# A graph layer's neighbour sums: gathered rows as three bfloat16 pieces, two dense blocks more, one-hots made three steps ahead

## The reference

```python
m_data = x[src] @ W_data.T + b_data
m_ctrl = x[src] @ W_control.T + b_control
msg = where(edge_type == 0, m_data, m_ctrl)
agg = segment_sum(msg, dst, num_segments=12500)
y   = x + relu(agg + x @ W_self.T + b_self)
out = (y - mean(y)) / sqrt(var(y) + 1e-5)        # per node, over the 128 features
```

## Time and profile before

| | |
|---|---|
| median of three runs | 3986.37 us (3984.35 to 3987.94) |
| the profiled execution | 3988.85 us |
| its span, first to last instruction | 3987.1 us |
| mean granted TensorE clock | 0.816 |
| busy share PE, POOL, DVE, ACT | 66%, 43%, 41%, 32% |
| DMA queue of the indirect gathers | 119.78 MB, 11.4% of 16 engines |

### The profile page before, as it was taken

One profiled execution on the slowest core, in us unless ns is written; L12 is line 12 of the kernel. 1 busy time (PEld: TensorE's weight loads), 2 busy tenths in 40 slices (PEclk: granted clock), 3 DMA queues, 4 the chain that ended last, 5 costly groups with the idle time before them and its releaser, 6 DMA issues.

```text
span 3987.1 us, 50434 instructions
## 1 busy us (share of the span) xinstructions
PE 2650.9 (66%) x19115; PEld 1498.6 (38%) x19115; DVE 1623.9 (41%) x3683; ACT 1267.6 (32%) x2283; POOL 1715.3 (43%) x1815
## 2 busy tenths in 40 slices
PE   3566676666766677666666666667666666767666
PEld 2333343333433344333333334334333333333334
DVE  7434344334443344434344343434334343443332
ACT  4233232333323333333333333333333333323332
POOL 6434444344443444444344443444444344444432
PEclk9878788888887888888787888878888787888878
DMA  5111111111111111111111111111111111111110
GB/s 163 50 32 34 35 32 37 32 36 35 34 36 32 36 34 37 34 34 36 33 36 34 34 35 34 35 35 34 36 34 36 32 36 34 34 37 31 37 34 26
DMA packets 112877, 151.17 MB, mean 38 GB/s; under 512 B 35545, under 2 KB 82712, under 8 KB 112632
## 3 DMA queue, kind: packets, MB, share of 16 engines
q0 software_dynamic: 58432, 119.78, 11.4%
q1 hardware_dynamic: 54200, 28.09, 2.5%
HBM read 138.99 MB, written 8.76 MB: 37 GB/s over the span
## 4 chain that ended last, share of the span: by engine, by line
another core or an unknown queue 39%; PE 36%; ACT 17%; issue 6%; DVE 1%; DVEq 0%; DMA 0%; SPq 0%; ACTq 0%
PE apply_ps L615 20%; ACT cnt L799 15%; PE sum_ps L581 6%; PE build L599 5%; PE misc L664 2%; PE misc L667 1%; PE misc L665 1%; PE misc L666 1%; ACT sg L782 1%; ACT std L824 0%; ACT zg L784 0%; PE misc L558 0%; DVE cnt L1074 0%; DVE hot_q L1063 0%
## 5 line engine op out<-in xcount | busy, mean ns | idle before, releaser
L517 POOL DMA_INDIRECT rows<-in_x,src_t x1760 | 1670.9, 949 | 2195.0 <-PE sum_ps L581 1694.1
L615 PE MATMUL apply_ps<-x,cnt 128*128 128x385 bf16 x8428 | 1753.4, 364 | 10.4 <-issue 10.3
L799 ACT ACTIVATE cnt<-build 128x784 bf16<-128x784 f32 x1376 | 1060.9, 817 | 1878.0 <-remote 1586.2
L599 PE MATMUL build<-hot_q,hot_p 64*128 64x196 bf16 x5504 | 452.8, 274 | 1226.0 <-ACT cnt L799 1104.6
L615 PEld LDWEIGHTS apply_ps<-x,cnt 128*128 128x128 bf16 x8428 | 908.9, 110 | 686.9 <-issue 294.3
L599 PEld LDWEIGHTS build<-hot_q,hot_p 64*128 64x128 bf16 x5504 | 194.3, 97 | 1509.8 <-issue 1338.4
L1063 DVE TENSOR_TENSOR hot_q<-const_ps,key_pq 128x784 bf16<-128x784 f32 x688 | 663.4, 964 | 0.0
L1063 DVE TENSOR_TENSOR hot_p<-const_ps,key_pq 128x512 bf16<-128x512 f32 x688 | 468.4, 681 | 134.4 <-remote 108.5
L1135 DVE SCALAR_TENSOR_TENSOR y_sb<-misc,x_u 128x128 f32<-128x128 f32 (+2 forms) x104 | 30.3, 292 | 1057.4 <-PE misc L667 896.6
L1108 DVE TENSOR_TENSOR acc_deg<-misc,acc_deg 2x32 f32 x352 | 63.1, 179 | 927.5 <-PE misc L624 652.4
L782 ACT ACTIVATE sg<-sum_ps 128x129 f32<-128x129 f32 x176 | 49.0, 279 | 774.2 <-PE sum_ps L581 758.1
(11 more groups left out here) (174 smaller groups left out, 1063.5 us busy)
## 6 DMA issues: line engine op xcount, KB each, us to landing
rows<-in_x,src_t POOLq DMA_INDIRECT x1760
cnt<-in_x SPq DMA_DIRECT2D x13, 448.0 KB
x_u<-in_x SPq DMA_DIRECT2D x42, 64.0 KB
out<-out_sb SPq DMA_DIRECT2D x42, 64.0 KB
key_dram<-fin SPq DMA_DIRECT2D x12, 192.0 KB
x_u<-in_x SPq DMA_DIRECT2D x40, 53.5 KB
out<-out_sb SPq DMA_DIRECT2D x40, 53.5 KB
win_i<-in_dst SPq DMA_DIRECT2D x22, 64.0 KB, 2.0
```

Of the source, the lines that this page charges most:

```text
L517: pool.indirect_dma_start(out=rows[:, slot, 0:D], out_offset=None, in_=x, in_offset=bass.IndirectOffsetOnAxis(ap=src_t[:, col:col + 1], ax ...
L599: last = pe.matmul(build_ps[z][:, o:o + 2 * XBLOCKS], hot_p[half, slot, :], hot_q[half, slot, :], start=True, stop=True)
L615: last = pe.matmul(apply_ps[:, 0:385], cnt[:, k % 2, b, :], x3[:, b, 0:385], start=(b == 0), stop=(b == XBLOCKS - 1))
L799: act.activation(o, i.rearrange("p h (m b) -> p b h m", b=XBLOCKS), ACT.Copy).then_inc(evacuated, 1)
```

## The change

- `BLOCKS` 86 to 88, `GATHER_0` 1365 to 1395: two more dense blocks (704 batches), 173 rounds of gathered tiles in place of 176. 173 rounds are laid on 177 places (0 to 176); places 23, 67, 111 and 155 hold none.
- From round 12 on (`F32_ROUNDS = 12`) a gathered row has the three bfloat16 pieces: 384 elements, 768 bytes, from a copy of `x3` in DRAM (`x3_dram`), against 512 bytes of float32 before. ACT's queue stores this copy in 15 DMAs in steps 6 to 13.
- The sum of such a round is ten bfloat16 matmuls of 385 columns, with `hot` in bfloat16 (`hot_b`). DVE adds the three pieces out of PSUM (`add_parts`) in the place of ACT's `take_sums`.
- `AHEAD` 3 to 2: 20 slots; round r is issued once the sum of round r - 2 is signalled.
- `make_onehots` of the dense nodes is three steps ahead of `build` in place of two, in the same ring of four: at step s it makes those of step s + 3 and waits for the build of step s - 1. One more batch is made before step 0.
- Jobs, turns and outputs of units get their steps from one list (`place` takes the next free step), so a unit's turn or output can fall on another step of its place: by that list 70 outputs stand in q3 (63 before) and 24 turns in q3 (none before).
- There are 718 steps in place of 704; the last sum is at step 704, and the last block is applied in steps 704 to 711.

```diff
-BLOCKS = 86
+BLOCKS = 88
-GATHER_0 = 1365
+GATHER_0 = 1395
-SLOTS = 30
-AHEAD = 3
+SLOTS = 20
+F32_ROUNDS = 12
+ROW = 3 * D
+AHEAD = 2
...
+    places = (BATCHES + APPLY_AT) // 4 - (0 if BLOCKS == 86 else 1)
+    spare = places - PAIRS
+    left_out = {2 * ((places * (2 * i + 1) // (2 * spare)) // 2) + 1 for i in range(spare)}
+    gather_step = [4 * j for j in range(places) if j not in left_out][:PAIRS]
+    sum_step = [place(s + 1) for s in gather_step]
...
+                if ps == F32_ROUNDS:
+                    pool.wait_ge(x3_stored, 16 * (XCH + 1))
                 for i in range(2 * GT):
...
+                    early = ps < F32_ROUNDS
                     pool.indirect_dma_start(
-                        out=rows[:, slot, 0:D], out_offset=None, in_=x,
+                        out=rows_f[:, slot, 0:D] if early else rows[:, slot, 0:ROW],
+                        out_offset=None, in_=x if early else x3_dram,
...
-                if ps % 8 == (4 if ps > 8 else 5) and ps // 8 + 1 < KGROUPS:
-                    gather_keys(ps // 8 + 1)
+                if ps in key_round:
+                    gather_keys(key_round[ps])
...
+                    if ps < F32_ROUNDS:
+                        last = pe.matmul(sum_ps[part, 0:D + 1], hot[:, ps % 3, st, :], rows_f[:, slot, 0:D + 1],
+                                         start=(j == 0), stop=(j == GT - 1))
+                    else:
+                        last = pe.matmul(sum_ps[part, 0:ROW + 1], hot_b[:, ps % 3, st, :], rows[:, slot, 0:ROW + 1],
+                                         start=(j == 0), stop=(j == GT - 1))
                 last.then_inc(rows_used, 1)
...
+            def store_x3(c):
+                full = XB if c < XCH - 1 else XB - 1
+                act.wait_ge(x3_ready, c + 1)
+                act.dma_start(x3_dram[c * XB * P:(c * XB + full) * P, :].rearrange("(b p) d -> p b d", p=P),
+                              x3[:, c * XB:c * XB + full, 0:ROW]).then_inc(x3_stored, 16)
...
-                if q == 0 and ps < PAIRS:
-                    take_sums(ps)
+                if gather_at.get(s, PAIRS) < F32_ROUNDS:
+                    take_sums(gather_at[s])
...
+            def add_parts(ps):
+                dve.wait_ge(rows_used, ps + 1)
+                dve.tensor_tensor(zg[:, ps % 2, :], t_mask[:, 0, :], sum_ps[:, ROW:ROW + 1].to_broadcast([P, 2]),
+                                  ALU.mult)
+                dve.tensor_reduce(sg[:, ps % 2, 0:D], sum_ps[:, 0:ROW].rearrange("p (k d) -> p d k", k=3), AX.X,
+                                  ALU.add).then_inc(sg_ready, 1)
...
+            make_onehots(2)
...
-                if batch_at(s + 2) is not None:
-                    make_onehots(batch_at(s + 2))
+                if batch_at(s + 3) is not None:
+                    make_onehots(batch_at(s + 3))
```

More of the change, by code:

```diff
@@ L74, in gnn_resnorm @@
         cut = [n0 + (n1 - n0) * i // k for i in range(k + 1)]
+        end = sum_step[min(EPOCH * (e + 1), PAIRS) - 1]
         for i in range(k):
[L76 to L81, removed]
+            t, o = ((9, 10), (11, 15), (19, 23))[i]
+            wanted.append((end + t, Unit(cut[i], cut[i + 1] - cut[i], end + t, end + o, False, e % 2, cut[i] - base)))
+    tail_wanted = [w for w in wanted if w[1].n0 == DENSE - P or w[0] >= sum_step[-1] + 5 and not w[1].dense]
+    ends = [w[1] for w in tail_wanted]
+    TAIL = len(ends)
+    assert TAIL == 4 and ends[0].dense and not any(v.dense for v in ends[1:])
+    units = []
+    for s, v in sorted((w for w in wanted if w not in tail_wanted), key=lambda w: w[1].out):
+        s = place(max(s, units[-1].turn + 1 if units else 0))
+        units.append(v._replace(turn=s, out=place(max(s + 1, v.out, units[-1].out + 1 if units else 0))))
+    assert all(b.turn > a.out for a, b in zip(units, units[2:]))
     UNITS = len(units)
@@ L85, in gnn_resnorm @@
     assert len(turn_at) == UNITS and len(out_at) == UNITS
[L86 to L107, removed]
+    for v in units:
+        if not v.dense:
+            e = (v.n0 - WIN_0) // EPOCH_NODES
+            assert e + 2 >= EPOCHS or v.out + 2 < sum_step[EPOCH * (e + 2) - 1]
+        else:
+            u = v.n0 // P
+            assert v.out < block_step[min(2 * u + 4, BLOCKS - 1)]
+    TURN_END = BATCHES + 3
+    STEPS = max(taken) + 4
+    gather_at = {s: r for r, s in enumerate(gather_step)}
+    sums_at = {s: r for r, s in enumerate(sum_step)}.get
+    keys_at = {s: g for g, s in key_step.items()}.get
+    ptr_at = {s: g for g, s in ptr_step.items()}.get
+    block_turn_at = {s: k for k, s in enumerate(block_step)}.get
+    hot_at = {gather_step[r - 2] + 2: r for r in range(2, PAIRS)}
+    epoch_at = {sum_step[EPOCH * (e + 1) - 1] + 1: e for e in range(EPOCHS - 1)}
+    key_round = {min(r for r in range(PAIRS) if gather_step[r] >= s + (12 if g == 1 else 16)): g
+                 for g, s in ptr_step.items()}
     def posted_at(s):
@@ L874, in _ @@
                     act.wait_ge(end_turned, 1)
-                    act.activation(end_xt, build_ps[0][:, 0:TAIL * P].rearrange("p (j r) -> p j r", r=P),
-                                   ACT.Copy).then_inc(end_xt_ready, 1)
+                    for j, v in enumerate(ends):
+                        last = act.activation(end_xt[:, j, 0:v.r], build_ps[0][:, j * P:j * P + v.r], ACT.Copy)
+                    last.then_inc(end_xt_ready, 1)
             act.wait_ge(end_mv_ready, 1)
@@ L1101, in add_sums @@
                 e = ps // EPOCH
[L1102 removed]
+                dve.wait_ge(misc_full, job[sum_step[ps]] + 1)
                 for g in range(2):
@@ L1193, in _ @@
                     post(posted_at(s))
+                if F32_ROUNDS <= gather_at.get(s, 0):
+                    add_parts(gather_at[s])
                 if sums_at(s) is not None:
```

133 lines of the change are left out of this document (82 added, 51 removed).

## The result

The changed kernel takes **3942.34 us** (median of 4 runs, 3936.33 to 3944.66) against 3986.89 (4 runs): ratio 0.989, interval 0.9875 to 0.990. It is 44 us faster; I had said 7 us faster, 3980, with a range from 3945.

What follows compares the result with a forecast made beforehand. A closed circle through POOL's gathers and PE's late q2 signals was taken as the bound; -11 - 22.6 + 55 - 48 + 24 + 11 - 15.3 = -6.9 gave 3980 us, range 3945 to 4060.

Steps and rivals of the forecast that it cites:

- What bounds the kernel: Mid-run places: closed circle of sum, ten POOL gathers, late release of PE's q2 signals, copy, build, apply; 22.5 us each.
- Landing: Behind POOL's last gather: 768-byte rows delay the release by 0.15 us in each of 161 rounds, +24 us.
- Sum: Sum closing each place: paired bfloat16 matmuls take 1.0 us, saving 0.3 us in 161 rounds, -48 us.
- rival 1: After the release: the clock's return takes back the shorter sum, so the -48 falls away; 4004 us, chance 0.08.
- Places, units: Mid-run: one place less -22.6, five without gathers +55 (11.0 us each); outputs and turns moved into q3 +11 us.
- The clock's doubt: After the release in each place: time at half clock may shift, 0.15 us on average, 25 us in all.
- End: Behind the last place's sum: 40.9 us against 56.2, -15.3 us, with 19 of apply and 17.5 of old end chain.
- Start: First rounds: two rounds ahead makes POOL pause and lets PE's signals through; -11 us, bounds 0 and -18.
- one-hots: DVE's make_onehots three steps ahead: no effect, since PE never waits for them mid-run; zero, bounds -5 and +10.
- 2: Places with an output in q0: late signals reach q1, PE stops at q2; +220, 4200 us, chance 0.06.
- 3: In the sum: bfloat16 pairs don't overlap, 0.83 us in 161 rounds, +134; 4114 us, chance 0.05.
- 4: In POOL's gather row: pauses let PE's signals through, up to 830 us go; about 3150 to 3900, chance 0.07.

Runs made afterwards that it cites:

- the made hold: Waits on a chip without PE's late signals delay ACT's copy of q2's build until the round's gathers land: kernel before 3954.0 us, against 2315.0 without waits.
- emu_after: Changed kernel with waits that delay ACT's copy of q2's build until the gathers land: 3938.4 us, 0.996 of the kernel before with the same waits.
- emu_places86: Changed kernel with 86 blocks, 176 rounds and no empty place, plus waits delaying ACT's copy of q2's build until the gathers land: 3895.9 us.
- after2: The changed kernel itself, run again on a chip where PE's signals weren't late: 2328.0 us, 1.0081 of the kernel before.
- before2: The kernel before, unchanged, traced on a chip where PE's signals weren't late: 2310.1 us.

## Why the prediction was off

*What bounds the kernel*: right, and shown by the made hold. My sentence "PE's signals of q2 don't get through" was too narrow, as PE's instructions stand as well. What I didn't foresee at all is that the hold belongs to the chip, or to its condition: in four of six sets of runs the same program runs in 2310 to 2315 us.

*Landing* (+24) is the step that failed: the release was taken to wait for the rows' landing and so to grow with the row. Its size came from one place with keys, and I took the wrong copy there. These rows of POOL and ACT stand before those two:

```profile
2252.40 0.94 POOL L517 DMA_INDIRECT rows<-in_x,src_t  x1 [0.30 <-issue]
...
2255.45 0.82 ACT L799 ACTIVATE cnt<-build 128x784 bf16<-128x784 f32 x1 [10.17 <-remote]
```

The release is the copy at 2255.45, 2.11 us behind the last row gather (2253.34) and 0.38 us before the last key gather has ended; the copy at 2258.26, from which I had the 2.43, is the second one of q2 and has waited 1.99 us. In the first runs' traces the release doesn't grow (2.18 and 2.11 us, and 3.01 to the second copy in both), although the last gather's rows land 1.40 us behind its end before and 1.46 after: 0 in place of +0.15 us a place, 24 of the 37 us. The Trainium skill (DMA: Bandwidth & Descriptors, Anatomy of one DMA) gives an estimated 0.075 us more for 32 KB more. The landing agrees with that (+0.06 here, +0.10 in the made hold); the real release does not follow it.

*Sum* (-48): mechanism right, pairs overlap. The Trainium skill (TensorEngine Tiling (Array Packing), Key Properties) says that different tiles load weights and multiply in parallel; the 1.01 us for five pairs agree. In the traces the sum shrinks from 1.43 us on average to 1.06 from round 12 on, -59 in 161 rounds, since one old sum in five ran over 1.5 us and two took 5.7 and 4.1. In the made hold the bfloat16 rounds are worth only 37 us (0.17 us a place in the traces), because later landing (0.10 us a place) and POOL's slightly longer gathers (0.04) go against the shorter sum (-0.29); from the release to the sum both versions have 6.43 us. So rival 1, the clock taking the shorter sum back, did not come.

*Places, units*: an empty place costs 11.1 us more, as forecast (11.0), and the fifth, with the last sum, 13.6. Moved turns and outputs cost 0.06 us a place, 9 us, for which I had 11.

*The clock's doubt* (0.15 us a place, 25 us) had about the right size: emu_after and emu_places86 differ by 0.17 us a place, and where turns, outputs and keys fall is all that I know to differ inside one. In the change itself the part behind the release grows by 0.06 us in the first runs' traces (5.65 to 5.71) and by as much in the made hold (5.66 to 5.72). The made hold shortens a place by 0.14 us (22.55 to 22.41) where the first traces show 0.27; 0.10 of the difference is the landing that the made hold pays.

*End* (-15.3): nineteen microseconds of apply came as forecast (last apply ends at 3929.4). The 17.5 us that I carried over from the old end were too long: its end units ran at a granted clock of 0.50 (0.64 us a pair of matmuls, now 0.38 at 1.00), and from the stores' issue to the end of the span it had 10.6 us against 5.7 now. Only argued: POOL's last drain of its transfers takes 9.1 us in the old trace and 2.2 in the new.

*Start* (-11) and *one-hots* (0) held. The lead's third step showed no effect that the intervals can tell, without the hold (2324.6 and 2328.0 in two sets) or with it (3785.9 and 3775.2 in one).

*Rivals*: 1, 2 and 3 didn't come; 4 came when made on purpose, and to less time (2816) than the 3150 that I gave it at best.

## What to carry to other kernels

Where the chain shows a large share from an unknown source, look at what another engine issues in a row at that time, and break the row up: three waits of POOL in a round, for work that is due anyway, took 27% off with the hold, and one such wait cost nothing without it. When a term is read from a single place, make sure that the row is the same event: a copy that another engine's build has released isn't the release. Make a suspected stall by waits on a quiet chip: that prices each term when the real stall can't be called up. And take both kernels to more than one chip: here the sign of the change depends on it.

## What was unexpected of the hardware

- The same program takes 2310 to 2315 us on four chips and 3842 to 3987 on a fifth and in the first runs. POOL's gathers take 949 and 951 ns in the two traces, ACT's copies 817 and 818; PE and its signals are what is held up.
- With the hold, while POOL issues gathers 1.25 us apart, a signal that PE gives 2.7 us after the first gather comes at once, and one given 5.5 us after it comes 2.07 us behind the last (the place shown above). PE runs on for a few us and then moves only some matmuls at a time. A gap of 1.69 us was enough to clear it. DVE's signals are not held in that stretch. Why is open: the profile doesn't tell whether PE is stopped itself or gets its instructions late, nor what tells the chips apart.
- Stores of 9.6 MB at the start delay SP's transfers to `key_dram`, which the dense keys wait for (median 3.6 us from issue to landing in after2, 2.2 in before2), and with them round 5 by some 17 us (142 against 125.5); ten steps later rounds 6 to 8 are slower instead, and 7 us are left of the gain.
